# Cross attention's first head group in two halves, and the batch loop written out

## The reference, cut to what matters

```python
cq = heads(ci @ cq_w, NH, CHD)            # NH = 16 heads of CHD = 8 features
ckv = encoder_outputs @ ckv_w             # 1601 context rows
ck, cv = jnp.split(ckv, 2, axis=-1)
cctx = sdpa(cq, ck, cv, causal=False)     # softmax(q k / sqrt(8)) v
hidden_states = hidden_states + cctx @ cdense_w
```

## Time and profile before

| | us |
|---|---|
| median of three runs (2340.41 to 2343.27) | 2342.53 |
| the profiled execution: its time | 2338.46 |
| the profiled execution: span from the first to the last instruction | 2336.5 |
| PE busy in the span | 2001.2 |
| DVE, ACT, POOL busy | 1299.6, 922.0, 766.5 |
| mean granted TensorE clock | 0.911 of full |

### The profile page before, as it was taken

One profiled execution on the slowest core, in us unless ns is written; L12 is line 12 of the kernel. 1 busy time (PEld: TensorE's weight loads), 2 busy tenths in 40 slices (PEclk: granted clock), 3 DMA queues, 4 the chain that ended last, 5 costly groups with the idle time before them and its releaser, 6 DMA issues.

```text
span 2336.5 us, 34832 instructions
## 1 busy us (share of the span) xinstructions
PE 2001.2 (86%) x11932; PEld 1480.0 (63%) x11932; DVE 1299.6 (56%) x2036; ACT 922.0 (39%) x1718; POOL 766.5 (33%) x676
## 2 busy tenths in 40 slices
PE   3999787898799978799889988879888997886986
PEld 2776576556676657655677756755577775774655
DVE  6666245655666523575566652467457663346733
ACT  1555132470355413256045541326515552231731
POOL 3788310001287821000237870100025876110000
PEclk8999898799899989879899998988989998897998
DMA  4000200201000010100100001020000001102000
GB/s 174 13 8 7 108 1 1 82 2 48 27 10 12 37 75 1 50 33 6 43 27 13 8 37 75 1 81 1 22 29 26 10 8 65 46 1 81 1 1 5
DMA packets 17612, 74.58 MB, mean 32 GB/s; under 512 B 2320, under 2 KB 9744, under 8 KB 13968
## 3 DMA queue, kind: packets, MB, share of 16 engines
q1 hardware_dynamic: 16848, 69.55, 8.1%
q10 hardware_dynamic: 576, 2.62, 0.3%
HBM read 71.12 MB, written 1.05 MB: 31 GB/s over the span
## 4 chain that ended last, share of the span: by engine, by line
PE 69%; DVE 16%; issue 7%; ACT 5%; POOL 1%; DMA 0%; SPq 0%; DVEq 0%; ACTq 0%; POOLq 0%
PE x L860 28%; PE pv L860 18%; PE st L860 16%; PE mi L860 6%; DVE k_hi_lo L1473 2%; ACT k_hi_lo L633 2%; DVE prob_sums L1848 1%; DVE max_cross L1873 1%; DVE max_parts L1547 1%; DVE q_lo_shift L1556 1%; PE x L981 1%; ACT ck_stack L763 1%; DVE x_normed L1639 1%; DVE recip_sum L1755 1%; DVE recip_sum L1664 1%
## 5 line engine op out<-in xcount | busy, mean ns | idle before, releaser
L566 POOL TENSOR_TENSOR prob_sums<-prob_sums,probs 128x512 f32<-128x512 f32 x352 | 455.4, 1294 | 49.7 <-ACT probs L675 13.8
L675 ACT ACTIVATE probs<-st 128x512 f32<-128x512 f32 x416 | 228.2, 596 | 310.6 <-PE st L860 294.1
L1547 DVE TENSOR_REDUCE max_parts<-x 128x1 f32<-128x832 f32 x256 | 251.0, 1020 | 126.3 <-PE x L860 124.5
L549 POOL TENSOR_TENSOR rstd_work<-rstd_work 128x2 f32<-128x2 f32 x24 | 16.6, 693 | 829.4 <-DVE rstd_work L1470 829.4
L1873 DVE TENSOR_REDUCE max_cross<-x 128x1 f32<-128x512 f32 x384 | 238.5, 684 | 71.7 <-PE x L860 69.2
L860 PE MATMUL st<-q_hi_hi,k_hi_lo 128*128 128x256 f32 x832 | 231.4, 309 | 28.9 <-DVE q_lo_shift L1556 15.6
L860 PE MATMUL pv<-probs,v 128*64 128x256 f32 x1664 | 231.0, 396 | 3.7 <-DVE recip_sum L1664 3.7
L860 PEld LDWEIGHTS st<-q_hi_hi,k_hi_lo 128*128 128x128 f32 x832 | 159.6, 192 | 106.9 <-issue 97.7
L860 PE MATMUL st<-q_lo_shift,k_hi_rows 128*128 128x256 f32 x832 | 210.6, 285 | 0.0
L860 PE MATMUL x<-ck_stack,cq_blocks 128*128 128x512 f32 (+1 forms) x512 | 195.4, 454 | 0.9
L860 PEld LDWEIGHTS st<-q_lo_shift,k_hi_rows 128*128 128x128 f32 x832 | 160.5, 193 | 0.0
(11 more groups left out here) (289 smaller groups left out, 4143.1 us busy)
## 6 DMA issues: line engine op xcount, KB each, us to landing
w_gate_up<-in_wgu SPq DMA_DIRECT2D x4, 3072.0 KB, 10.0
w_ff<-in_w SPq DMA_DIRECT2D x8, 1024.0 KB, 5.9
w_qk<-in_wqk SPq DMA_DIRECT2D x4, 2048.0 KB, 8.3
w_pair<-in_w SPq DMA_DIRECT2D x32, 192.0 KB, 2.3
w_down<-in_wdn SPq DMA_DIRECT2D x4, 1536.0 KB, 13.3
w_dense<-in_wd SPq DMA_DIRECT2D x4, 1024.0 KB, 11.0
mask_ints<-in_mask SPq DMA_DIRECT2D x4, 832.0 KB, 4.3
ctx_t_raw<-in_ctxT SPq DMA_DIRECT2D x4, 832.0 KB, 6.1
```

The lines of the kernel that those rows point to most:

```text
L566: pool.tensor_tensor(acc[:, 0], acc[:, 0], prob[:, kt % 4], ALU.add).then_inc(add_pool.handle, 1)
L675: act.activation(prob[:, kt % 4], ST[kt % 2][:], ACT.Exp, scale=HD0 ** -0.5).then_inc(p_exp.handle, 1)
L1547: dve.tensor_reduce(mxs[:, qt, h, half:half + 1], X[n % 2][:].rearrange("p (c n) -> p c n", c=2)[:, :, 0:QUART], AX.XY, ALU.max).then_inc( ...
```

## The change

It has three parts.

1. The first group's maxima, shifts and scores come in two halves of two heads each. Parts 0 to 12 are those of heads 0 and 1, parts 13 to 25 those of heads 2 and 3 (`max_tile`). PE issues 13 + 5 = 18 parts, then the shifts of the first half (two copies on ACT), then tiles 0 to 12, which are the 13 key tiles of heads 0 and 1; then the shifts of the second half, and tiles 13 to 25. There are five shift steps for each entry instead of four. Ahead of tile 24 of a group PE issues the parts of the maxima that the next group's shift still lacks (`while g < ...`).
2. Value matmuls come in one running list, `done_pv`, four tiles at a time at every n with n % 4 == 3. The query tiles of group 2 are built behind tile 17 instead of tile 7.
3. All four entries are written out: `for b in range(B)` in place of the loop on each engine, and `passed` with all its increments is removed.

```diff
+        def score_tile(n):
+            gr, k = n // (2 * KT), n % (2 * KT)
+            return (gr, k % KT, k // KT) if gr == 0 else (gr, k // 2, k % 2)
+
+        def max_tile(g):
+            gr, m = g // CPARTS, g % CPARTS
+            if gr == 0:
+                m, h0 = m % (CPARTS // 2), m // (CPARTS // 2) * 2
+                if m == 12:
+                    return gr, [(qt, h0 + h) for qt in range(TT) for h in range(2)], 3
+                return gr, [(m // 6, h0 + m % 6 // 3)], m % 3
...
-                for g in range(CPARTS + LEAD):
+                for g in range(CPARTS // 2 + LEAD):
                     cross_max(g)
                 cross_shifts(0)
-                g = CPARTS + LEAD
...
+                pe.wait_ge(sc_set.handle, sc_set.at(b, 1))
+                g, done_pv = CPARTS // 2 + LEAD, 0
+                for n in range(8 * KT):
+                    gr, k = n // (2 * KT), n % (2 * KT)
+                    if n == KT:
+                        while g < CPARTS + LEAD:
+                            cross_max(g)
+                            g += 1
+                        cross_shifts(1)
+                        pe.wait_ge(sc_set.handle, sc_set.at(b, 2))
+                    elif k == 0 and gr:
+                        pe.wait_ge(sc_set.handle, sc_set.at(b, gr + 2))
+                    if k == 24 and gr < 3:
+                        while g < CPARTS * (gr + 2) + LEAD and g < 4 * CPARTS:
+                            cross_max(g)
+                            g += 1
+                        cross_shifts(gr + 2)
+                    cross_score(n)
+                    if g < 4 * CPARTS:
+                        cross_max(g)
+                        g += 1
+                    if gr < 2 and k == (17 if gr == 0 else 7):
+                        cross_queries(gr + 2)
...
+                    if n % 4 == 3:
+                        while done_pv < n - 3:
+                            cross_pv(done_pv)
+                            done_pv += 1
...
-            with pe.Fori(0, B - 1) as b:
-                body(b, True)
-            body(B - 1, False)
+            for b in range(B):
+                body(b, b < B - 1)
...
                     link(m)
-                    dve.sem_inc(passed.handle, 1)
                     for t in range(TT):
                         m = dve.bn_aggr(mv[:, t], bn[:, t])
...
                     pool.wait_ge(var_ready.handle, var_ready.at(b, n))
-                    pool.sem_inc(passed.handle, 1)
                     pool.tensor_tensor(rs[:, 2], rs[:, 0], rs[:, 1], ALU.pow).then_inc(rstd_ready.handle, 1)
```

More of the change, by code:

```diff
@@ L344, in program @@
         done = sig("batch_done", primed=True)
-        passed = sig("wait_passed")
         def prime(eng, *signals):
@@ L379, in st_bank @@
             return (ST[0][:], ST[1][:], half_bank(3))[n % 3]
+        def score_tile(n):
[8 more added lines that the diff above has]
+                return gr, [(m // 6, h0 + m % 6 // 3)], m % 3
+            qt, m = m // 13, m % 13
+            if m == 12:
+                return gr, [(qt, h) for h in range(4)], 3
+            return gr, [(qt, m // 3)], m % 3
         def slot(n):
@@ L428, in load_next @@
                 sp.wait_ge(w_split.handle, w_split.at(b * PAIRS + p - 1))
-                sp.sem_inc(passed.handle, 1)
                 load_pair(p)
@@ L610, in body @@
                 rsqrt(6)
-            with pool.Fori(0, B - 1) as b:
-                body(b, True)
-            body(B - 1, False)
+            for b in range(B):
+                body(b, b < B - 1)
         @block.scalar
@@ L813, in cross_queries, with cross_shifts @@
                     m.then_inc(qg_read.handle, 1)
-                def cross_shifts(gr):
-                    act.wait_ge(nmc_t.handle, nmc_t.at(b * 4 + gr))
-                    for h in range(4):
+                def cross_shifts(e):
+                    gr = max(0, e - 1)
+                    act.wait_ge(nmc_t.handle, nmc_t.at(b, e + 1))
+                    for h in ((0, 1), (2, 3))[e] if e < 2 else range(4):
                         m = act.activation(qb2[gr % 3][32 * h:32 * h + 4, h], MI[0:4, NT:2 * NT], ACT.Copy)
@@ L850, in body @@
                 memory_layer(1)
-            with act.Fori(0, B - 1) as b:
-                body(b, True)
-            body(B - 1, False)
+            for b in range(B):
+                body(b, b < B - 1)
         @block.tensor
@@ L1417, in body @@
+                while done_pv < 8 * KT:
+                    cross_pv(done_pv)
+                    done_pv += 1
                 pe.wait_ge(cc_read.handle, cc_read.at(b * 4 + 3))
@@ L1883, in body, with cross_max @@
-                for gr in range(4):
-                    cross_max(gr)
+                def cross_max(g):
+                    (gr, heads, c), bank = max_tile(g), max_bank(g)
+                    dve.wait_ge(mc2_mm.handle, mc2_mm.at(b, g + 1))
+                    (qt, h), (qt1, h1) = heads[0], heads[-1]
+                    if c < 3:
+                        t = dve.tensor_reduce(mxc[:, qt, h, c:c + 1], bank, AX.X, ALU.max)
+                    else:
+                        t = dve.tensor_reduce(mxc[:, qt:qt1 + 1, h:h1 + 1, 3],
+                                              bank[:, 0:4 * HEADW].rearrange("p (q h n) -> p q h n", q=qt1 - qt + 1, h=h1 - h + 1), AX.X, ALU.max)
+                    t.then_inc(mc2_read.handle, 1)
@@ new lines, in cross_shift @@
+                def cross_shift(e, g, h0, h1):
+                    dve.wait_ge(mc2_read.handle, mc2_read.at(b, g))
+                    if e:
+                        dve.wait_ge(nmc_t.handle, nmc_t.at(b, e))
+                    dve.tensor_reduce(nmx[:, :, h0:h1], mxc[:, :, h0:h1], AX.X, ALU.max, negate=True).then_inc(nmc.handle, 1)
+                    dve.wait_ge(nmc.handle, nmc.at(b, e + 1))
+                for g in range(4 * CPARTS):
+                    cross_max(g)
+                    if g + 1 == CPARTS // 2:
+                        cross_shift(0, g + 1, 0, 2)
+                    elif (g + 1) % CPARTS == 0:
+                        gr = g // CPARTS
+                        cross_shift(gr + 1, g + 1, 2 if gr == 0 else 0, 4)
@@ L1917, in body @@
                 assert count[0] == chain.per, count[0]
-            with dve.Fori(0, B - 1) as b:
-                body(b, True)
-            body(B - 1, False)
+            for b in range(B):
+                body(b, b < B - 1)
 _CONST = ("const_r", "const_f", "const_k")
```

117 lines of the change are left out of this document (35 added, 82 removed).

## The result

| | before | after |
|---|---|---|
| median of the runs | 2342.90 us (2340.41 to 2343.70, 4 runs) | 2370.48 us (2367.50 to 2373.09, 4 runs) |
| profiled execution, its span | 2338.46 us, 2336.5 us | 2368.11 us, 2366.3 us |
| mean granted clock | 0.911 | 0.923 |

The changed kernel is slower by 1.24%: the ratio of the times is 1.0124, with a 95% interval from 1.011 to 1.0138 (the medians alone differ by 27.6 us, 1.18%). The forecast was 2347.1 us with a range from 2330 to 2359; the time lies 11.5 us above that range.

The account below looks back on a forecast made before the run. PE was taken to bound the kernel, DVE's pace costing only where PE has nothing else to issue. 2338.46 + 18.0 - 8.8 - 4.6 = 2343.1, with 4.07 to the median 2347.1 us; range 2330 to 2359.

Parts of the forecast that it names:

- Sum for one entry: Cross attention of one entry, all its steps together: +4.5 us, between +1 and +7; +18.0 for four entries.
- (d): Hand-over to tile 26 without a value block to cover it: +1.0 us; later hand-overs, tiles 52 and 78: +0.5.
- (a): Opening of cross attention: first score earlier, since neg_max can follow 13 parts: -8.5 us.
- (f): Clock in cross attention: low level after the 15 parts loses 2.0 us, the opening's return 0.4: +2.4 (0 to 3.3).
- (b): Second half's shift behind tile 12: PE waits for ACT's exponential and two copies: +1.5 us (1.2 to 1.8).
- (c): Ahead of tile 24: 15 parts of maxima in a row without a tile between them, a stall of +8.1 us.
- (e): After tile 26 two fewer parts follow: -0.5 us; moving query tiles from tile 7 to 17 costs 0.
- the rival with a full clock: Clock stays full in the 15 parts ahead of tile 24: +2.1 us an entry, whole 2337.5; chance 0.22.
- The loop: Edges between entries, two loop edges removed at 4.4 us each: -8.8 us (-6.7 to -11.1).
- The increments: Removing increments of `passed` on DVE and POOL in normalisations saves 0.22 us, 21 times: -4.6 us (-2.5 to -5.3).
- the queue of waits is longer: More slow clock through group 1, worse phase at written-out edges: +7 us an entry, 3.4 an edge; 2359; chance 0.14.

Follow-up runs that it names:

- e1: The kernel before with its four entries written out on every engine, all increments of `passed` kept and group 0 whole; 2324.14 us.
- e2: The written-out kernel before (e1) with every increment of `passed` taken away, group 0 whole; 2333.24 us.
- e4: The kernel after with group 0's value matmuls written into four groups of 32 rows of PV instead of two, mixing heads' sums; 2350.74 us.
- e3: The kernel after with all increments of `passed` put back; 2365.09 us.
- e9: e8 with the maxima five behind every three score tiles up to tile 23, old value block places, and group 2's query tiles behind tile 18; 2327.80 us.
- e8: The kernel after with POOL's `rsqrt` increment back, halves by query tiles of four heads, and two maxima behind each of tiles 0 to 16; 2339.61 us.
- e10: The written-out kernel without increments (e2), with one put back, in POOL's `rsqrt`; 2324.02 us.
- e6: The kernel after with group 0 halved by query tiles, 128 queries of all four heads each, instead of by pairs of heads; 2356.77 us.

## Why the prediction was wrong

The decomposition by runs, beside the prediction's three terms:

| step | predicted | measured | from |
|---|---|---|---|
| entries written out | -8.8 | -16.4 | e1 against before |
| increments of `passed` | -4.6 | +9.1 | e2 against e1 |
| group 0 in halves | +18.0 | +34.9 | after against e2 |
| of it, groups of rows of PV | 0 | 17.4 | after against e4 |
| sum | +4.6 | +27.6 | |

By the intervals of the ratios e1 lies 9.8 to 19.4 us below before and e2 5.9 to 11.5, so the first two measured steps are known only to some 5 us each; the traces have them at the edges as -11.3 and +9.2. Of the 23.0 us between the two sums the halves hold 16.9, the increments 13.7, and the loop takes 7.6 back.

**The step that failed, cross attention.** The term missing from "Sum for one entry" is the slower value blocks of group 0: the sum has nothing for them. (d) read a block from the kernel before, about 1.1 us, and nothing in the sum let it change. Each of group 0's full blocks took 1.85 to the next load (1.00 in before). I had read `cross_pv` for when blocks are issued and not for where they write. With four groups written again, e4 leaves +3.2 to +4.0 an entry of my +4.5. That this is so near is in part luck: terms of both signs were off, as the list below shows.

The page "TensorE: Matmul & The Clock Gate" of the Trainium skill, section "Part 3: Packing small matmuls — row/col tiling", has matmuls with 32 output rows, each in a group of its own, run at the same time, and gives 2.38 times the rate for three groups. Every full block of before writes four, which hides that this is a condition. The runs here show two against four: 1.92 against 1.07 us.

**Its other terms, one by one.**

- (a), -8.5: right; the first score came 8.7 earlier. Not foreseen: the clock was full at once (1.00 from 438.00, in the row shown with e3) where before stayed at 0.50 for its first scores; by tile 4 that is another 1.4 us. (f) had +0.4 there.
- (b), +1.5: right. Tile 12 to 16 is 4.55 us in e4 and 3.06 before. After, 5.4, which holds a slow block too.
- (c), +8.1: right (its own 9.2 less 1.2 is 8.0). Tile 20 to 24 took 13.2 us in e4 and 4.7 before, 8.5 more; after has 9.3 more, with a block's 0.85 in it.
- (d), +1.5: too small. Tile 24 to 28 is 0.9 longer in e4 than before, and the way from there to the stage's end 2.0. e9, with the old places of the blocks, takes 2.4 us less than e8 from tile 24 to 36; its other pace of the maxima may have a part in that.
- (e), -0.5: not seen. The move of the query tiles costs 1.0 at tiles 16 to 20 (4.01 us in e4, 3.04 before) and gives back 0.5 at tiles 4 to 8.
- (f), +2.4: mis-sized. The low stretch is there, 6.8 us at 0.50 (1047.80 to 1054.60) in entries 1 to 3, and the rival with a full clock fell. In entry 0 it ends 3.4 us sooner, ahead of tile 24's exponential. There, 49.4 to 52.8 us into the stage, where the other entries are at 0.50:

```profile
471.00:474.40 3.40, 3.05 (x19) 1.44 (x19) 2.61 (x4) 2.92 (x7) 0.00 (x0) 1.00 0.00 0
```

Tiles 24 to 28 take 3.7 us in entry 0 and 4.6 in the others, so the longer stretch costs 0.9 where I had 2.0. The shorter one costs nothing that shows: the same tiles take 2.9 us in e4 with it and in e8 without any there. A low stretch at the stage's end, where the sum had no term, costs more. From the last exponential to x_b it is 8.9 us in entries 1 to 3 of after, at full clock, and 11.9 in entry 0:

```profile
538.00:546.50 8.50, 6.69 (x17) 5.38 (x18) 1.72 (x2) 0.05 (x1) 0.00 (x0) 0.60 0.00 0
```

These two make entry 0's stage 125.0 us and the others' 122.9.

**The loop.** The gaps of 6.5 us went, as forecast. The step that I discounted, from 5.5 to 4.4 an edge, needed no discount: e1's edges are 27.3, 5.6 less each at the two. The 365.03 us from which I took the discount are 27.3 for the edge and 337.7 for the way from the first attn_t to cq_hi, which was 335.6 in the loop's 368.40. That way varies between the entries of one kernel: after, all written out, has 337.7, 334.6, 334.6 and 337.9, with the clock at 0.50 for 55, 41, 41 and 48 us of it. So I read a difference of this kind as a cost of the loop's removal. Of the 5.7 us that e1's profile has less there, 3.4 are before's one long entry, and e1's profiled execution is the fastest of its five (2321.1 to 2330.1). How much of e1's further 5 us writing out really gives stays open.

**The increments.** Here the sign was wrong; this step failed too. I priced an instruction of 0.1 us by the gap that it makes, and asked nothing about what starts in that gap. Where the root's waiter on DVE and the next work of POOL both start when it is ready, the increment holds POOL's start back from 0.05 to 0.21 us behind DVE's, and that is worth 2.8 to 3.1 us at each of three edges. e10 shows that this one increment is the whole effect. On DVE the gap ahead of bn_aggr did shrink as forecast, from 0.15 to 0.04; on POOL the gap ahead of the power shrank from 0.18 to 0.14, 0.04 where I had taken 0.10. Neither gained anything that a run shows.

**The rivals.** None fits. The one that came closest, "the queue of waits is longer", had +7 an entry, near the 7.1 of three of after's entries, but from slow clock, and the 12.68 us against 9.85 are at full clock.

## What to carry to other kernels

When an order of tiles changes, look at which rows the small matmuls of one block write, not only at when the block comes: a block's duration read from the old order holds only if its mix of heads stays. Before removing an instruction that looks idle, look at what starts behind it on its own engine and on those released by the same event; a tenth or two of a microsecond can hold two engines apart. And an earlier start is worth little if the same work lies ahead of the next hand-over: sum up what the busiest engine must issue until then.

The versions that beat both kernels are the plain ones: before written out with its increments (2324.1 us) or with the one of them that matters (2324.0), and the mended halves level with them (2327.8).

## What the runs showed of the hardware

- Sixteen matmul rows of 32 outputs and 256 columns take 1.07 us into four groups of 32 rows of PSUM and 1.92 into two. Thirty-two of 128 columns into four groups take 1.08 (e6), no more than sixteen of 256:

```profile
442.58 1.08 PE L850 MATMUL pv<-probs,v_cross 128*32 128x128 f32 x32
```

- Two starts 0.05 us apart in place of 0.21 on DVE and POOL (e2 and e1) made DVE's next three pieces of work 0.4 to 1.0 us longer each, and an edge 3.1 us longer.
- Entries of one execution differ through the clock: in after the same tiles 24 to 28 took 3.7 and 4.6 us, and the end of the stage 8.9 and 11.9 us.
- The clock about the first scores came out at either level in kernels that differ little (0.50 in e3 and e6, 1.00 in after), each the same in all its entries. The runs do not settle what tips it.
